# Value products of four heads in 32-column tiles, with the softmax sums as a set of their own

## The chip, the cores and the metric

The kernel runs on one core of one Trainium2 chip. The metric is the device time of one execution in microseconds, the median of the runs.

## What is computed

One gated block of a Flamingo model, on `x` (4 x 512 x 512) and a context of 4 x 1601 x 512, in float32. Cut to what matters:

```python
x = x + jnp.tanh(g_xattn[0]) * mha(layernorm(x), ctx, ctx)     # 16 heads of 32, causal mask of -10000 instead of -inf
x = x + jnp.tanh(g_ffn[0])   * ffn(layernorm(x))
# mha:
scores = jnp.einsum('bhqd,bhkd->bhqk', qh, kh) / math.sqrt(hd)
scores = jnp.where(ki <= qi + (Sk - Sq), scores, -10000.0)
out = jnp.einsum('bhqk,bhkd->bhqd', softmax(scores), vh)
# ffn: rows and weights are rounded to 8-bit floats with a scale per row
t = silu(qx @ qwg.T * scales) * (qx @ qwu.T * scales)           # 512 -> 1408
y = quantized(t) @ qwd.T * scales                                # 1408 -> 512
```

## The kernel before

**The units of work.** The four batches with four groups of four heads each make 16 head groups (`gg`, `GALL = 16`; `NG` = 4 groups a batch, `GH` = 4 heads a group). Keys come in 13 tiles of 128 (`NT`, the last has 65), queries in one row of 512 columns. A group has 26 steps (`STEPS`); in one step the engines do, for one key tile and two heads, the scores (`scores`, L842, with the causal masks of the late tiles at L848), the exps (`exps`, L632, ScalarE) and, two steps later (`LAG = 2`), the value products (`values`, L866). Steps 0 to 12 are the first head pair, 13 to 25 the second. Late key tiles (t = 9 to 12) need fewer query columns: 449, 321, 193, 65.

**Scores** are products of 97 rows: the keys and queries of a head are split in a high and a low 16-bit part, and stacked by DMA (`put_heads`, L335 and L336, 24 copies a group from `kTh`, `kTl`, `qTh`, `qTl`), with a row that holds the shift, minus the maximum of the query's scores (`put_shift`, L340, row `mrow`). The scores of the two heads go to PSUM banks 0 and 1, each in two halves of 64 key columns (`HALVES`), so that two matmuls with 64 columns each share the array. The second use of a bank waits for the exp that reads it (`ex_done`).

**Values** are 32-bit products: the values of a head and a column of ones (33 columns, `VW`), times the exps; the ones give the sum of the softmax. The two heads of a step write partitions 0 to 32 and 64 to 96 of bank 2 or 3. After 13 steps `out_copy` (L622) copies the 97 rows to `oT`, `out_turn` (L823) transposes them, and `join_out` (L1099 to L1112, VectorE) adds the masked part and divides; `add_update` (L460, GpSimd) adds it to `xs`. That is done twice a group, at steps 4 and 17 of the counts that follow.

**The shift** needs the maximum of every score ahead of time. So with each step goes a maximum job for a later group (`max_turn`, L780, two heads of 32 rows at once, masks at L785; `AHEAD = 6`), reduced by VectorE (`max_reduce`, L1069). Its keys are prepared by transposes (`stage_turn`, L767 and L759, at steps 10, 13 and 19), a cast (`stage_high`, L592) and a subtraction (`stage_low`, L1060). The masked values' sums are the suffix products (`suffix_turn`, L808 to L813, step 8).

**The feed-forward part** goes along in the same steps: first the quantization of the weights (`weight_*`, in groups 0 to 3), then, from group 4, one tile of 128 rows per group: transposes at step 20, four up products (`up_turn`, L887) at steps 22, 24, 0 and 2, the hidden transposes (L898) at 12 and the down product (`down_turn`, L910) at 14.

**What sets the order.** Every engine runs its own program over the same step counter `at`; the place of a job in it is written out by hand:

```python
for at in range(END):                       # TensorE, before
    ...                                     # stage_turn, out_turn, suffix_turn, max_turn, shift_turn
    if gg < GALL:
        scores(pe, gg, u)
    if LAG <= at < LAST + LAG:
        values(pe, (at - LAG) // STEPS, (at - LAG) % STEPS)
    ...                                     # row tiles, weights
```

Maximum, stage, suffix, turn, row tile and weight jobs share two bank pairs (banks 4 to 7) in the order in which they are numbered; `free_slot` makes a job wait for whoever reads the pair's last one (`dve_free`, `act_free`). SP issues all loads and copies in one queue.

Of the kernel before, what the change touches and what calls it, by code (L numbers as in the profile page):

```python
# [5 lines left out]
def flamingo_gated_block(nc, x_d, ctx_d, gx_d, gf_d, wg_d, wu_d, wd_d, didx_d, out_d):  # L6
# [9 lines left out]
    P = 128  # L16
# [13 lines left out]
    VW = HD + 1  # L30
# [10 lines left out]
    NP = 6  # L41
    LAG = 2
# [6 lines left out]
    HALVES = ((0, P // 2), (P // 2, P))  # L49
    assert IT * P == I and DT + QT == NT - 1  # L50
# [113 lines left out]
    with ExitStack() as ctx:  # L164
# [26 lines left out]
        vf = sb("vf", [P, NT, H, VW])  # L191
        ksrc = sb("ksrc", [P, NT, P])
        xlg = sb("xlg", [P, QT, P])
        kTh, kTl = sb("kTh", [P, 2, SK], f16), sb("kTl", [P, 2, SK], f16)
        qTh, qTl = sb("qTh", [P, 2, S], f16), sb("qTl", [P, 2, S], f16)
# [5 lines left out]
        pr = sb("pr", [P, NP, S])  # L201
        oT = sb("oT", [P, S])
# [12 lines left out]
        cmb = sb("cmb", [P, QT, 2, HD])  # L215
        upd = sb("upd", [P, QT, 2, HD])
        den = sb("den", [P, 2, QT, 2])
# [12 lines left out]
        t_q = (t_q0[:, :], pr[:, 0:2, :].rearrange("p a n -> p (a n)").bitcast(bf16)[:, 0:I])  # L230
        t_T = (t_T0[:, :], pr[:, 2:4, :].rearrange("p a n -> p (a n)").bitcast(bf16)[:, 0:I])
# [37 lines left out]
        gate_mm, gate_th, ps_clear = sem("gate_mm"), sem("gate_th"), sem("ps_clear")  # L269
# [3 lines left out]
        dve_s, ones_in, vones_in = sem("dve_s"), [sem("ones_in0"), sem("ones_in1")], sem("vones_in")  # L273
# [10 lines left out]
        o_ev, o_tr, upd_ready, xs_done = sem("o_ev"), sem("o_tr"), sem("upd_ready"), sem("xs_done")  # L284
# [11 lines left out]
        def unit(gg, u, j):  # L296
            return 2 * (gg * STEPS + u) + j

# [29 lines left out]
        def put_heads(sp, gg, i):  # L328
            s = gg % 2
            if gg >= 2:  # L330
                sp.wait_ge(qk_mm, unit(gg - 2, i * NT + NT - 1, 1) + 1)
            for r in (2 * i, 2 * i + 1):
                rows = slice(HD * r, HD * r + HD)
                for part in range(3):
                    sp.dma_start(kst[s][HD * part:HD * part + HD, r, :], (kTh, kTl, kTh)[part][rows, s, :]).then_inc(stk[s][r], 16)  # L335
                    sp.dma_start(qst[s][HD * part:HD * part + HD, r, :], (qTh, qTh, qTl)[part][rows, s, :]).then_inc(stk[s][r], 16)  # L336
# [11 lines left out]
        def _(sp):  # L348
# [9 lines left out]
            for i in range(PAIRS):  # L358
                put_heads(sp, 0, i)
# [7 lines left out]
            for i in range(PAIRS):  # L367
                put_heads(sp, 1, i)
            for gg in range(GALL):
# [10 lines left out]
                if g == NG - 1 and b + 1 < B:  # L380
                    for t in range(4):
                        load_values(sp, b + 1, t)
# [3 lines left out]
                if g == NG - 1 and b + 1 < B:  # L386
                    for t in range(4, 8):
# [3 lines left out]
                if g == NG - 1 and b + 1 < B:  # L391
                    load_values(sp, b + 1, 8)
                    load_values(sp, b + 1, 9)
                if gg + 2 < GALL:
                    put_heads(sp, gg + 2, 1)
                if g == NG - 1 and b + 1 < B:
# [58 lines left out]
        def add_update(pool, pp):  # L455

            b, h = pp // (NG * PAIRS), 2 * (pp % (NG * PAIRS))
            cols = slice(h * HD, (h + 2) * HD)
            pool.wait_ge(upd_ready, pp + 1)
# [33 lines left out]
        def _(pool):  # L493
# [22 lines left out]
            nc.gpsimd.memset(vf[:, :, :, HD:VW], 1.0).then_inc(vones_in, 1)  # L516
            pool.wait_ge(consts, 15)
            pool.wait_ge(vones_in, 1)
# [99 lines left out]
        def out_copy(act, pp):  # L618
            act.wait_ge(pv_done, 2 * (pp + 1) * NT)
            if pp >= 1:  # L620
                act.wait_ge(o_tr, pp)
            nc.scalar.copy(oT[0:64 + VW, :], ps[0:64 + VW, 2 + pp % 2, :]).then_inc(o_ev, 1)  # L622

        def exps(act, gg, u):
            t = u % NT
            kn, q0 = KT[t][1], Q0[t]
            for j in range(2):
                n = unit(gg, u, j)
                act.wait_ge(qk_mm, n + 1)
                if n >= NP:  # L630
                    act.wait_ge(pv_done, n - NP + 1)
                nc.scalar.activation(pr[0:kn, n % NP, q0:S], ps[0:kn, j, q0:S], ACT.Exp, scale=SCALE).then_inc(ex_done, 1)  # L632

# [56 lines left out]
        def _(act):  # L690
# [12 lines left out]
            for at in range(END):  # L703
                gg, u = divmod(at, STEPS)
                if gg + 2 < GALL and u in STAGE_AT:
                    stage_high(act, gg + 2, STAGE_AT[u])
                if gg < GALL:
                    exps(act, gg, u)
                if turned_at(at + 2) is not None:
                    out_copy(act, turned_at(at + 2))  # L710
# [26 lines left out]
        def free_slot(pe, job):  # L737

            before = before_in_bank[job]
            if before is None:  # L740
                if banks[job] < 4:
                    pe.wait_ge(ex_done, 2 * LAST)
                    pe.wait_ge(o_ev, GALL * PAIRS)
# [53 lines left out]
        def suffix_turn(pe, gg):  # L797
# [9 lines left out]
            for a, e in HALVES:  # L807
# [471 lines left out]
```

## Time and profile before

| | |
|---|---|
| median of 3 runs | 1160.27 us (1158.86 to 1160.71) |
| profiled execution | 1161.19 us, its span 1159.4 us |
| mean granted TensorE clock | 0.949 of full speed |
| TensorE (PE) busy | 970.5 us, 7770 instructions |
| VectorE (DVE) | 859.7 us, 1438 |
| ScalarE (ACT) | 656.5 us, 1343 |
| GpSimd (POOL) | 332.1 us, 350 |

The busy time of an engine is the time in which at least one of its instructions runs; matmuls overlap, so a busy PE need not be at its peak. A 32-bit matmul stands in the trace as two instructions. The groups begin some 65 us after the start and end near 1041 us; after that come the last row tiles alone.

### The profile page before, as it was taken

To read this page: it belongs to the slowest core of one execution; us is meant where nothing else is said; L and a number is where in the kernel's file an instruction comes from. 1 tells how busy PE (TensorE), PEld (TensorE's weight loads), DVE (VectorE), ACT (ScalarE), POOL (GpSimd) and SP (SyncE) were. 2 spreads that over 40 slices of the span, in tenths; PEclk is the share of its full clock that TensorE was granted. 3 is DMA by queue.
4 is the path that set the end of the run, shared out by engine and by line. 5 is a ranking of instruction groups with operands and counts; after the bars stand their busy time and mean duration, and the time that the engine had idled before them with its cause. 6 is when DMAs were issued, how large, how long until landed. Compare 5 with 4: busy or idle time off the path is not lost.

```text
span 1159.4 us, 21085 instructions
## 1 busy us (share of the span) xinstructions
PE 970.5 (84%) x7770; PEld 399.4 (34%) x7770; DVE 859.7 (74%) x1438; ACT 656.5 (57%) x1343; POOL 332.1 (29%) x350
## 2 busy tenths in 40 slices
PE   4588889888879989999889999998899999984344
PEld 2233333333323334343334333333333343432222
DVE  7768789887747888777677877787778786446764
ACT  2165567675646666666556666665566666753321
POOL 3012323332101414132323232222314132443343
PEclk9998899999989999999999999999999999996766
DMA  7942423230572221114812121218421110000000
GB/s 147 154 122 69 115 66 93 66 86 26 112 88 57 66 57 39 53 43 83 124 41 60 63 61 36 51 41 115 70 61 35 27 41 10 2 10 10 10 10 19
DMA packets 155119, 70.69 MB, mean 61 GB/s; under 512 B 111032, under 2 KB 142856, under 8 KB 155016
## 3 DMA queue, kind: packets, MB, share of 16 engines
q1 hardware_dynamic: 153256, 63.57, 26.5%
q0 software_dynamic: 1760, 5.77, 1.8%
q8 instruction: 62, 1.02, 0.4%
q14 instruction: 41, 0.34, 0.1%
HBM read 39.08 MB, written 4.19 MB: 37 GB/s over the span
## 4 chain that ended last, share of the span: by engine, by line
PE 42%; DVE 36%; issue 10%; ACT 4%; POOL 4%; DMA 2%; SPq 1%; POOLq 0%; DVEq 0%; ACTq 0%
DVE mch L1069 17%; PE ps L866 13%; PE ps L842 8%; PE ps L887 6%; PE ps L780 5%; PE ps L910 3%; DVE ff L985 2%; DVE ff L981 2%; DVE ff L989 2%; PE ps L785 2%; ACT pr L632 1%; DVE upd L1112 1%; DMA qst<-mrow 1%; PE ps L848 1%; DVE cmb L1102 1%
## 5 line engine op out<-in xcount | busy, mean ns | idle before, releaser
L632 ACT ACTIVATE pr<-ps 128x512 f32<-128x512 f32 (+4 forms) x832 | 397.2, 530 | 250.0 <-PE ps L842 125.1
L1069 DVE TENSOR_REDUCE mch<-ps 128x2 f32<-128x1024 f32 (+4 forms) x416 | 432.3, 1056 | 69.2 <-PE ps L780 32.8
L866 PE MATMUL ps<-pr,vf 128*33 128x512 f32 (+4 forms) x1664 | 380.6, 537 | 0.0
L842 PE MATMUL ps<-qst,kst 97*64 97x512 f16 (+4 forms) x1600 | 250.5, 371 | 18.0 <-DMA qst<-mrow 11.4
L780 PE MATMUL ps<-kTh,qTh 32*128 32x512 f16 (+4 forms) x832 | 156.2, 373 | 59.2 <-DVE mch L1069 40.7
L780 PEld LDWEIGHTS ps<-kTh,qTh 32*128 32x128 f16 x832 | 39.5, 92 | 279.0 <-DVE mch L1069 106.9
L842 PEld LDWEIGHTS ps<-qst,kst 97*64 97x64 f16 (+1 forms) x1600 | 77.3, 111 | 108.0 <-ACT pr L632 57.4
L866 PEld LDWEIGHTS ps<-pr,vf 128*33 128x33 f32 (+1 forms) x1664 | 86.8, 113 | 56.6 <-issue 4.9
L1141 DVE SCALAR_TENSOR_TENSOR ff<-ps,scs,wsb 128x352 f32<-128x352 f32 x56 | 32.6, 583 | 73.1 <-PE ps L887 73.1
L448 POOL TENSOR_TENSOR t_q<-ff 128x768 bf16<-128x768 f32 (+1 forms) x28 | 47.4, 1694 | 100.1 <-DVE ff L989 100.1
L887 PE MATMUL ps<-wgu,t_T 128*64 128x352 bf16 x768 | 66.5, 316 | 0.0
L429 POOL TENSOR_TENSOR ff<-ff,wsb 128x352 f32<-128x352 f32 x48 | 46.0, 957 | 64.0 <-DVE ff L1141 64.0
L1060 DVE TENSOR_TENSOR kTl<-ps,kTh 128x1024 f16<-128x1024 f32 (+1 forms) x32 | 31.7, 992 | 41.0 <-ACT kTh L592 40.8
L848 PE MATMUL ps<-maskT,idb 128*64 128x128 bf16 (+2 forms) x576 | 61.7, 214 | 0.0
L989 DVE TENSOR_TENSOR ff<-ff 128x512 f32<-128x512 f32 (+3 forms) x66 | 55.0, 833 | 2.1
L659 ACT ACTIVATE ff<-ps,scs 128x352 f32<-128x352 f32 x48 | 26.6, 554 | 52.2 <-PE ps L887 52.2
L453 POOL TENSOR_TENSOR xs<-xs,ff 128x512 f32<-128x512 f32 x14 | 17.8, 1273 | 132.1 <-DVE ff L1179 132.1
L887 PEld LDWEIGHTS ps<-wgu,t_T 128*64 128x64 bf16 x768 | 44.3, 111 | 32.6 <-issue 20.8
L460 POOL TENSOR_TENSOR xs<-xs,upd 128x256 f32<-128x256 f32 x32 | 24.0, 749 | 107.9 <-DVE upd L1112 107.9
L433 POOL TENSOR_TENSOR ff<-ff 128x352 f32<-128x352 f32 x48 | 51.7, 1078 | 3.8
L489 POOL TENSOR_TENSOR cw<-w,count 128x16 f32<-128x16 f32 x16 | 3.9, 245 | 165.9 <-ACT w L615 165.9
L785 PE MATMUL ps<-idb,maskT 128*64 128x128 bf16 (+2 forms) x640 | 47.1, 229 | 0.0
(151 smaller groups left out, 1198.2 us busy)
## 6 DMA issues: line engine op xcount, KB each, us to landing
kst<-kTh SPq DMA_DIRECT2D x128, 100.1 KB, 2.2
ksrc<-in_ctx SPq DMA_DIRECT2D x16, 768.0 KB
vf<-in_ctx SPq DMA_DIRECT2D x48, 256.0 KB, 5.1
kst<-kTl SPq DMA_DIRECT2D x64, 100.1 KB, 2.2
xs<-in_x SPq DMA_DIRECT2D x16, 256.0 KB, 4.8
qst<-qTh SPq DMA_DIRECT2D x128, 32.0 KB, 1.9
out<-xs SPq DMA_DIRECT2D x16, 256.0 KB, 2.0
ff<-in_L_ffn_w_down SPq DMA_DIRECT2D x4, 704.0 KB, 4.4
```

The lines of the kernel that those rows point to most:

```text
L429: nc.gpsimd.tensor_tensor(t_u[e][:, cols], t_u[e][:, cols], wsb[:, I + c * CW:I + (c + 1) * CW], ALU.mult).then_inc(gated, 1)
L433: nc.gpsimd.tensor_tensor(t_u[e][:, cols], t_u[e][:, cols], t_g[e][:, cols], ALU.mult).then_inc(gu_ready, 1)
L448: nc.gpsimd.tensor_tensor(t_q[e][:, cols], t_v[e][:, cols], t_m[e][:, cols], ALU.subtract).then_inc(qt_ready, 1)
L632: nc.scalar.activation(pr[0:kn, n % NP, q0:S], ps[0:kn, j, q0:S], ACT.Exp, scale=SCALE).then_inc(ex_done, 1)
L780: last = nc.tensor.matmul(slot(job)[:, 512 * i:512 * i + k1 - k0], qTh[rows, gg % 2, qt * P:(qt + 1) * P], kTh[rows, gg % 2, k0:k1], start ...
L785: last = nc.tensor.matmul(slot(job)[a:e, 512 * i + lo - k0:512 * i + hi - k0], maskT[:, a:e], idb[:, lo - d0:hi - d0], start=False, stop=True)
L842: last = nc.tensor.matmul(ps[a:e, j, q0:S], kst[s][0:ST, r, k0 + a:k0 + e], qst[s][0:ST, r, q0:S], start=True, stop=(t < DT))
L848: last = nc.tensor.matmul(ps[a:e, j, q0:q0 + n_m], idb[:, a:e], maskT[:, m0:m0 + n_m], start=False, stop=True)
L866: nc.tensor.matmul(ps[64 * j:64 * j + VW, 2 + pp % 2, q0:S], vf[0:kn, t, h, :], pr[0:kn, n % NP, q0:S], start=(t == 0), stop=(t == NT - 1) ...
L887: last = nc.tensor.matmul(ps[a:e, bank(job) + side, 0:CW], qxT[:, k, a:e], wgu[:, k, side * I + c * CW:side * I + (c + 1) * CW], start=(k ...
L989: return nc.vector.tensor_tensor(v, v, m, ALU.add)
L1069: nc.vector.tensor_reduce(mch[:, qt, 2 * hp:2 * hp + 2, c], both[:, :, 0:k1 - k0], AX.X, ALU.max).then_inc(dve_free, 1)
```

## The change

Steps alternate between the head pairs: steps 2t and 2t + 1 do key tile t for heads 0, 1 and 2, 3. The value products of key tile t are done for all four heads at once in step 2t + 3, each in 32 columns of the array and without the column of ones, into bank 2. The sums are a set of four products with ones as weights (`prob_sums`), into bank 3, at the start of step 2t + 4. The exps have room for three key tiles of four heads. There is one turn, one join and one update a group (128 columns), at step 4; bank 2 and bank 3 are each copied by ScalarE (`out_copy`, `sums_copy`), now ahead of the exps of their step, and the sums are turned by four small products. Scores, suffix, up and down products are cut in `QUARTERS` of 32 columns; the maximum jobs keep 64-column masks. `kTl` and `qTl` have one buffer instead of two, so `stage_low` waits for the copies of the group before, and all 24 head copies of a group are issued at one place, behind the value loads and the shift row. `dynamic_dma_scratch_size` is set to 2048.

```diff
+    QUARTERS = tuple((P // 4 * i, P // 4 * (i + 1)) for i in range(4))
+    TILE_SLOTS = 3
...
     def turned_at(at):
-        pp, rest = divmod(at - 4, NT)
-        return pp - 1 if rest == 0 and 1 <= pp <= GALL * PAIRS else None
+        gg, u = divmod(at, STEPS)
+        return gg - 1 if u == 4 and 1 <= gg <= GALL else None
+    def values_at(at):
+        gg, u = divmod(at - 3, STEPS)
+        return (gg, u // 2) if u % 2 == 0 and 0 <= gg < GALL else None
+    def added_at(at):
+        gg, u = divmod(at - 4, STEPS)
+        return (gg, u // 2) if u % 2 == 0 and 0 <= gg < GALL else None
...
         def load_values(sp, b, t):
-                last = unit(b * NG - 1, STEPS - NT + t, 1)
-                sp.wait_ge(pv_done, last + 1)
+                sp.wait_ge(pv_done, value_count(b * NG - 1, t))
...
-                if gg + 2 < GALL:
-                    sp.wait_ge(dve_free, dve_count["stage", gg + 2, 0])
-                    put_heads(sp, gg + 2, 0)
...
                 if gg + 1 < GALL:
                     put_shift(sp, gg + 1)
...
                     for t in range(10, NT):
                         load_values(sp, b + 1, t)
+                if gg + 2 < GALL:
+                    sp.wait_ge(dve_free, dve_count["stage", gg + 2, 0])
+                    put_heads(sp, gg + 2)
...
         def exps(act, gg, u):
+            t, i = divmod(u, PAIRS)
+            kn, q0, k = KT[t][1], Q0[t], NT * gg + t - TILE_SLOTS
+            if k >= 0:
+                act.wait_ge(sums_done, k + 1)
             for j in range(2):
...
         def scores(pe, gg, u):
-            i, t = divmod(u, NT)
+            t, i = divmod(u, PAIRS)
...
                 if n >= 2:
                     pe.wait_ge(ex_done, n - 1)
-                for a, e in halves:
+                quarters = [(a, min(e, kn)) for a, e in QUARTERS if a < kn]
+                for a, e in quarters:
...
+        def values(pe, gg, t):
+            pe.wait_ge(ex_done, exp_count(gg, t, PAIRS - 1))
+            for r in range(GH):
+                last = nc.tensor.matmul(ps[HD * r:HD * (r + 1), 2, q0:S], vf[0:kn, t, g * GH + r, :], prob(gg, t, r)[0:kn, q0:S],
+                                        start=(t == 0), stop=(t == NT - 1))
+            last.then_inc(pv_done, 1)
+        def prob_sums(pe, gg, t):
+            for r in range(GH):
+                last = nc.tensor.matmul(ps[HD * r:HD * (r + 1), 3, q0:S], onesf[0:kn, 0:HD], prob(gg, t, r)[0:kn, q0:S],
+                                        start=(t == 0), stop=(t == NT - 1))
+            last.then_inc(sums_done, 1)
...
         def stage_low(dve, gg, part):
+            if gg >= 1 and part == PARTS[0]:
+                for r in range(GH):
+                    dve.wait_ge(stk[(gg - 1) % 2][r], ((gg - 1) // 2 + 1) * STK)
```

The order on TensorE, steps 4 to 6 of a group from 4 on. Before (maximum job L780, scores L842, values L866):

```order
L780 MATMUL ps<-kTh,qTh 128x512 x2
L842 MATMUL ps<-qst,kst 64x512 x4
L866 MATMUL ps<-pr,vf 33x512 x2
L780 MATMUL ps<-kTh,qTh 128x512 x2
L842 MATMUL ps<-qst,kst 64x512 x4
L866 MATMUL ps<-pr,vf 33x512 x2
```

Now (turn L837 and L840, maximum job L795, scores L860, values L878, sums L888):

```order
L837 MATMUL ps<-idf,oT 128x128 x4
L840 MATMUL ps<-idf,oS 128x4 x4
L795 MATMUL ps<-kTh,qTh 128x512 x2
L860 MATMUL ps<-qst,kst 32x512 x8
L795 MATMUL ps<-kTh,qTh 128x512 x2
L860 MATMUL ps<-qst,kst 32x512 x8
L878 MATMUL ps<-pr,vf 32x512 x4
L888 MATMUL ps<-pr,onesf 32x512 x4
L795 MATMUL ps<-kTh,qTh 128x512 x2
```

Values stood behind the scores of every step; now a set of values and a set of sums stand together behind the odd step, and between the even and the odd scores there is only a maximum job.

The same around the key transposes of step 10, before (transposes L767):

```order
L866 MATMUL ps<-pr,vf 33x512 x2
L767 MATMUL ps<-idf,ksrc 128x128 x8
L780 MATMUL ps<-kTh,qTh 128x512 x2
L842 MATMUL ps<-qst,kst 64x321 x2
L848 MATMUL ps<-maskT,idb 64x128 x2
```

and now (transposes L782, masks of the maximum job L800):

```order
L888 MATMUL ps<-pr,onesf 32x512 x4
L782 MATMUL ps<-idf,ksrc 128x128 x8
L795 MATMUL ps<-kTh,qTh 128x512 x2
L860 MATMUL ps<-qst,kst 32x512 x8
L795 MATMUL ps<-kTh,qTh 128x449 x2
L800 MATMUL ps<-idb,maskT 64x128 x4
L860 MATMUL ps<-qst,kst 32x512 x8
L878 MATMUL ps<-pr,vf 32x512 x4
```

The second maximum job behind the transposes, which uses their bank pair, has lost the values ahead of it.

## Rows read from the trace of the kernel before

**Rows 1.** The page: busy time, share and instructions of each engine
```profile
PE 970.5 (84%) x7770; PEld 399.4 (34%) x7770; DVE 859.7 (74%) x1438; ACT 656.5 (57%) x1343; POOL 332.1 (29%) x350
```

**Rows 2.** One stretch: PE, PEld, DVE, ACT, POOL busy (x), PEclk, DMA share, GB/s
```profile
443.00:503.00 60.00, 56.74 (x482) 23.10 (x482) 47.04 (x76) 38.33 (x78) 16.86 (x20) 1.00 0.18 47
```

**Rows 3.** The page's chain that ended last, by engine
```profile
PE 42%; DVE 36%; issue 10%; ACT 4%; POOL 4%; DMA 2%; SPq 1%; POOLq 0%; DVEq 0%; ACTq 0%
```

**Rows 4.** PE timeline: start us, us, engine, line, operation, tiles and forms
```profile
665.67 0.39 PE L780 MATMUL ps<-kTh,qTh 32*128 32x512 f16 x2
665.99 0.62 PE L842 MATMUL ps<-qst,kst 97*64 97x512 f16 x4
666.44 1.03 PE L866 MATMUL ps<-pr,vf 128*33 128x512 f32 x4
667.40 0.55 PE L823 MATMUL ps<-idf,oT 97*128 97x97 f32 x4
667.88 0.39 PE L780 MATMUL ps<-kTh,qTh 32*128 32x512 f16 x2
```

**Rows 5.** PE timeline of masked steps, same columns
```profile
647.44 0.41 PE L842 MATMUL ps<-qst,kst 97*64 97x512 f16 x2
647.71 0.38 PE L842 MATMUL ps<-qst,kst 97*64 97x512 f16 x2
654.55 0.30 PE L785 MATMUL ps<-idb,maskT 128*64 128x128 bf16 x4
654.69 0.26 PE L842 MATMUL ps<-qst,kst 97*64 97x193 f16 x2
```

**Rows 6.** PE timeline around one quarter of a row tile's up product
```profile
681.61 1.36 PE L887 MATMUL ps<-wgu,t_T 128*64 128x352 bf16 x16
682.90 0.39 PE L780 MATMUL ps<-kTh,qTh 32*128 32x512 f16 x2
```

**Rows 7.** PE and ACT timeline of two steps that follow closely
```profile
659.54 0.60 PE L842 MATMUL ps<-qst,kst 97*64 97x512 f16 x4
659.96 2.27 ACT L632 ACTIVATE pr<-ps 128x512 f32<-128x512 f32 x4 [0.31 <-PE ps L842]
660.72 0.79 PE L842 MATMUL ps<-qst,kst 97*64 97x512 f16 x4
661.34 0.28 PE L866 MATMUL ps<-pr,vf 65*33 65x65 f32 x4
```

**Rows 8.** Groups by form: the cast and the subtraction of a 1024-column key part
```profile
L592 ACT CAST kTh<-ps 128x1024 f16<-128x1024 f32 x16 | 16.2, 1013 | 10.0 <-PE ps L767 10.0
L1060 DVE TENSOR_TENSOR kTl<-ps,kTh 128x1024 f16<-128x1024 f32 x16 | 19.6, 1226 | 13.6 <-ACT kTh L592 13.6
```

**Rows 9.** PE timeline, waits that return in every group (idle time in brackets)
```profile
466.55 0.39 PE L780 MATMUL ps<-kTh,qTh 32*128 32x512 f16 x2 [0.76 <-DVE mch L1069]
491.20 0.39 PE L780 MATMUL ps<-kTh,qTh 32*128 32x512 f16 x2 [1.01 <-DVE mch L1069]
526.34 0.39 PE L780 MATMUL ps<-kTh,qTh 32*128 32x512 f16 x2 [0.76 <-DVE mch L1069]
```

**Rows 10.** Waits: us in total, times, longest; and PE group L808 by form
```profile
PE ps L842 <- DMA qst<-mrow: 11.4, 3, 5.7
L808 PE MATMUL ps<-vf,later 128*64 128x512 f32 x64 | 17.1, 611 | 5.1 <-POOL vsum L485 4.0 <-DVE mch L1069 1.1
```

**Rows 11.** SP timeline before the second batch: head copies and shift row
```profile
306.70 0.58 SPq L335 DMA_DIRECT2D kst<-kTh  x1
307.33 0.59 SPq L336 DMA_DIRECT2D qst<-qTh  x1
319.53 1.54 SPq L340 DMA_DIRECT2D qst<-mrow  x1
```

**Rows 12.** PEld group of the up product by form
```profile
L887 PEld LDWEIGHTS ps<-wgu,t_T 128*64 128x64 bf16 x768 | 44.3, 111 | 32.6 <-issue 20.8
```

More of the change, by code:

```diff
@@ L297, in unit, with exp_count, value_count, prob @@
             return 2 * (gg * STEPS + u) + j
+        def exp_count(gg, t, i):
+            return unit(gg, PAIRS * t + i, 1) + 1
+        def value_count(gg, t):
+            return NT * gg + t + 1
+        def prob(gg, t, r):
+            i, j = divmod(r, 2)
+            return pr[:, PAIRS * ((NT * gg + t) % TILE_SLOTS) + i, j, :]
         def load_x(sp, b):
@@ L357, in _ @@
             sp.wait_ge(dve_free, dve_count["stage", 0, 0])
-            for i in range(PAIRS):
-                put_heads(sp, 0, i)
+            put_heads(sp, 0)
             for t in range(3, NT):
@@ L366, in _ @@
             sp.wait_ge(dve_free, dve_count["stage", 1, 0])
-            for i in range(PAIRS):
-                put_heads(sp, 1, i)
+            put_heads(sp, 1)
             for gg in range(GALL):
@@ L380, in _ @@
                 if g == NG - 1 and b + 1 < B:
-                    for t in range(4):
-                        load_values(sp, b + 1, t)
-                if gg + 2 < GALL:
-                    sp.wait_ge(dve_free, dve_count["stage", gg + 2, 0])
-                    put_heads(sp, gg + 2, 0)
-                if g == NG - 1 and b + 1 < B:
-                    for t in range(4, 8):
+                    for t in range(10):
                         load_values(sp, b + 1, t)
@@ L742, in free_slot @@
                     pe.wait_ge(ex_done, 2 * LAST)
[L743 removed]
+                    pe.wait_ge(o_ev, GALL)
+                    pe.wait_ge(sums_ev, GALL)
                 return
@@ L815, in suffix_turn, with out_turn @@
             last.then_inc(suf_mm, 1)
-        def out_turn(pe, pp):
-            job = ("turn", pp)
+        def out_turn(pe, gg):
+            job = ("turn", gg)
             free_slot(pe, job)
-            pe.wait_ge(o_ev, pp + 1)
-            n = 64 + VW
+            pe.wait_ge(o_ev, gg + 1)
             for qt in range(QT):
-                last = nc.tensor.transpose(slot(job)[:, qt * n:(qt + 1) * n], oT[0:n, qt * P:(qt + 1) * P], idf[0:n, 0:n])
+                nc.tensor.transpose(slot(job)[:, qt * P:(qt + 1) * P], oT[:, qt * P:(qt + 1) * P], idf[:, :])
+            pe.wait_ge(sums_ev, gg + 1)
+            for qt in range(QT):
+                last = nc.tensor.matmul(slot(job)[:, S + GH * qt:S + GH * (qt + 1)], oS[:, qt * P:(qt + 1) * P],
+                                        idf[:, :].rearrange("p (h d) -> p h d", h=GH)[:, :, 0], start=True, stop=True)
             last.then_inc(o_tr, 1)
         def scores(pe, gg, u):
-            i, t = divmod(u, NT)
+            t, i = divmod(u, PAIRS)
             k0, kn = KT[t]
@@ L885, in up_turn @@
                 for k in range(DC):
-                    for a, e in HALVES:
+                    for a, e in QUARTERS:
                         last = nc.tensor.matmul(ps[a:e, bank(job) + side, 0:CW], qxT[:, k, a:e],
@@ L940, in _ @@
                 gg, u = divmod(at, STEPS)
+                if added_at(at) is not None:
+                    prob_sums(pe, *added_at(at))
                 if gg + 2 < GALL and u in STAGE_AT:
@@ L952, in _ @@
                     scores(pe, gg, u)
-                if LAG <= at < LAST + LAG:
-                    values(pe, (at - LAG) // STEPS, (at - LAG) % STEPS)
+                if values_at(at) is not None:
+                    values(pe, *values_at(at))
                 for n, k in tiles_at(at):
@@ L1088, in suffix_weigh, with join_out @@
                                     ALU.mult).then_inc(dve_free, 1)
-        def join_out(dve, s, pp):
-            gg, i = divmod(pp, PAIRS)
-            k, n = gg % 2, 64 + VW
-            got = slot(("turn", pp))[:, 0:QT * n].rearrange("p (t n) -> p t n", t=QT)
-            sums = [got[:, :, HD + 64 * j] for j in range(2)]
-            dve.wait_ge(o_tr, pp + 1)
+        def join_out(dve, s, gg):
+            got = slot(("turn", gg))
+            update = upd[:, :, :, :].rearrange("p t h d -> p (t h d)")
+            heads = upd[:, :, :, :].rearrange("p t h d -> p (t h) d")
+            dve.wait_ge(o_tr, gg + 1)
@@ L1096, in join_out @@
             dve.wait_ge(cw_ready, gg + 1)
             dve.wait_ge(dve_free, dve_count["suf", gg])
-            for j in range(2):
-                s.step(nc.vector.tensor_tensor(den[:, 0, :, j], cw[:, k, :, 2 * i + j], sums[j], ALU.add))
-            for j in range(2):
-                h = 2 * i + j
-                ins = nc.vector.tensor_tensor(cmb[:, :, j, :], got[:, :, 64 * j:64 * j + HD], sw[:, :, h * HD:(h + 1) * HD], ALU.add)
-                if j == 0:
-                    s.step(ins)
-            s.settle()
@@ new lines, in join_out @@
+            if gg >= 1:
+                dve.wait_ge(xs_done, gg)
+            s.step(nc.vector.tensor_tensor(update, got[:, 0:S], sw[:, :, :].rearrange("p t n -> p (t n)"), ALU.add))
+            s.settle()
+            nc.vector.reciprocal(den[:, 1, :, :], den[:, 0, :, :]).then_inc(dve_free, 1)
+            dve.wait_ge(dve_free, dve_count["turn", gg])
+            nc.vector.scalar_tensor_tensor(heads, heads, tg[:, 0:1],
+                                           den[:, 1, :, :].rearrange("p t h -> p (t h)").unsqueeze(2).broadcast_to([P, QT * GH, HD]),
```

135 lines of the change are left out of this document (55 added, 80 removed).

## The prediction

> **What bounds the kernel now.** I read the busy times first: TensorE (PE) 970.5 us of the 1159.4 us span, VectorE (DVE) 859.7, ScalarE (ACT) 656.5 [rows 1]. The chain that ended last names PE for 42% and DVE for 36% [rows 3], so the two take turns. The stretch view tells more: in 60 us, just over one head group of the steady part, PE is busy for 56.74 at full clock (1.00, the 2.4 GHz level), DVE for 47.04, ACT for 38.33 [rows 2]. One group takes 526.34 - 466.55 = 59.8 us, by the same wait in two groups that follow each other [rows 9]. So PE sets the pace there, and some 3 us a group are its waits. What counts is therefore what one step puts on PE, and what PE waits for.
>
> **One quiet step now** [rows 4], by the starts: maximum job 0.32 us (665.67 to 665.99), scores 0.45, values 0.96, then the next job: 1.74 us in all. The streams are 512/2.4 = 213 ns for the maximum job, 2 x 213 = 427 for the scores, and 853 for the values, if the 32-bit pass takes twice that for each of two passes and two heads share the array. What is left is about 0.11 us behind the maximum job and behind the values, where the shape of the array tile changes, and 0.03 behind the scores, where it does not. Two steps: 3.48 us.
>
> **What the new tiles save on PE: nothing.** Before, 4 heads x 1 key tile are two value sets of two heads, 2 x 0.853. Now they are one set of four value products and one set of four sums, again 2 x 0.853. Scores, suffix, up and down products are cut in four instead of two, twice the instructions with as many streamed sets. The changes of tile shape per two steps stay at four (sums to maximum, to scores, to maximum, to scores). So the sum is made of what follows, per group of 26 steps and against the profiled execution's 1161.2 us (the median of the three runs is 0.9 lower).
>
> **a. The exps come into the path.** Between the scores of an even step and those of the odd step there are no values any more, only a maximum job, and both steps use the same two score banks. How soon scores can follow scores is seen where the values were short: scores at 659.54 and exps of 1.08 us a pair from 659.96; the next scores start at 660.72, sit there for the second exp, and the values behind them start at 661.34, 1.80 us after the first scores [rows 7]. Without that wait it would be 0.43 + 0.11 + 0.32 + 0.45 = 1.31. A quiet pair then takes 1.80 + values 0.86 + sums 0.96 + maximum 0.32 = 3.94 us against 3.48: **+0.46**. Pairs with an up or down product, with a transpose job in the middle or with narrow late key tiles don't pay it: the row tiles' jobs all fall on even steps, between the two scores. Quiet are steps 4/5, 6/7 and 8/9: +1.4 a group.
>
> **b. Steps 10/11.** The key transposes of step 10 hand their bank pair to a cast of 1.01 us and a subtraction of 1.23 [rows 8]; with the hand-overs it is free some 2.5 us later. The maximum job of step 11 wants that pair. With values in between it came 1.74 later or more; now it stands ahead of everything after 0.85, waits 1.6 us, and the scores of step 11 and the values are queued behind it. In return the present wait of 0.76 at this place [rows 9] goes, since values and sums now stand together ahead of the transposes: +0.9. In steps 12/13 (the hidden transposes and their two copies) and 16/17 (masks) I estimate the same mechanism at +0.7 together, between 0 and 1.5.
>
> **c. One more change of tile shape.** The masks of the maximum jobs keep 64 columns; behind them the scores went on after 0.14 us [rows 5]. Now scores have 32: +0.11 in each of 10 masked jobs: +1.1.
>
> **d. Short instructions.** Two masks of 63 columns cost 647.71 - 647.44 - 0.213 = 57 ns [rows 5], so 28 ns an instruction, weights included, where the stream needs 26 for both. Four of them: 112 ns. For 12 heads with 128-column masks (now 4 in 0.14 us, about 60 ns a head) +0.6, for 4 with 63 +0.2, for the 65-key tile (6 instructions a head for 2) +0.5, narrow values and sums +0.2: +1.5. Below it is 0, if the instructions overlap more. An up product is no such case: a set now has 2 in 147 ns (16 in 1.29 - 0.11) [rows 6], and 4 x 28 = 112 still fits.
>
> **e. Turning the result.** Twice four transposes of 0.48 and a shape change [rows 4], 1.2 us, become four, and four sum turns of two passes each with 128 weight columns: between 8 x 0.03 and 8 x 0.12; I take 0.7, nearest to the transposes that load as many columns: +0.1. DVE's join is done once instead of twice, and at step 4 only; ACT copies as often as before, now ahead of the exps of steps 2 and 3, where up products cover it. If those were gone, it would be 0.6 a copy.
>
> a to e: 1.4 + 0.9 + 0.7 + 1.1 + 1.5 + 0.1 = 5.7 us, in the 11 groups 4 to 14: **+63**. Group 15 has no maximum jobs, so scores follow scores at once and wait longer: **+6**. Groups 0 to 3 carry the weight work, with more PE waits for DVE; there c and d (2.6) and a are half hidden: 2.5 each, **+10**.
>
> **f. What is relieved.** The join no longer stands in DVE's queue around step 17, ahead of the waits near step 21; of the 1.01 [rows 9] most stays, since two maximum jobs now stand close together; I take 0.5 a group: **-5.5**. At the three batch starts PE waits 11.4 us for the shift row and 4.0 for the value sums [rows 10]. The shift row was queued on SP behind value loads and 12 head copies of 0.63 each (306.70 to 307.33), and went out at 319.53 [rows 11]. Now a value tile comes free every two steps from step 3 on, the loads spread over the group, and the head copies stand behind the shift row. I take all of it and half a microsecond more: **-16**. The 24 head copies then start with the new group and take 24 x 0.63 = 15 us, and the new wait of the subtraction in step 10, 23 us into the group (10/26 of 59.8), finds them landed. Late next at these places is ACT's shift copy.
>
> Sum: 1161.2 + 63 + 6 + 10 - 5.5 - 16 = 1218.7; I forecast **1217 us** against the median.
>
> **Rivals.**
> **B, faster (12%).** The relief wins. If ACT's release does not hold the odd scores, that is if they may start within 0.85 us of the even ones, a and b go, and so do d and the extra in groups 0 to 3 and 15. Left are c and e, 1.2 x 11 = 13, less 5.5 and 16, and less the restart of PE after the three stops, some 5: 1161 - 13 = 1148. For it: the waits at the batch starts are real. Against it: rows 7 show the stall in this very kernel.
> **C, PE limited by the number of instructions (12%).** 6817 matmuls become 11425 by the order of the programs. If each of the 4608 added, with its weight load, costs 28 to 30 ns on the path, it is +135 in place of d's 20: 1217 + 115 = 1330; if half do, about 1275. For it: 28 ns is measured only where loads are few. Against it: in the up product 16 loads with a mean of 111 ns, 1.78 us, lie within 1.18 [rows 6, 12], so loads of whole columns hide beside the streams. The Trainium skill (TensorE: Matmul & The Clock Gate, "The mechanism") says that a weight load overlaps running matmuls only if its row group differs. By that rule all 128-row loads here would stand in the path, and this rival would be the likeliest; rows 6 and 12 speak against it.
> **D, four tiles don't run four wide (3%).** No row shows more than two. At two wide each step pays 0.43 for scores and 0.85 for values and sums again; over 416 steps, at a mean width of 0.85 of 512, that is +450: 1670.
> **E, the head copies come late (2%).** If SP is held for over 5 us more, the subtraction of step 10 waits and the maximum jobs behind it, some 3 us a batch start: 1226, within my range.
>
> **Numbers.** The forecast has 71%, its own range is 1165 (d zero, the estimates of b zero, groups 0 to 3 unchanged) to 1260 (b and groups 0 to 3 doubled). The range of 1150 to 1275 takes in the half of C that is milder and the upper edge of B. About 0.2% can be told from no change here. Faster: B, 0.12. Same: 0.02, between B and the low end. Slower: the rest, 0.86.
>
> **What would show it.** a: in steps 4 to 9 scores-to-values 1.8 us apart over the pair, with waits for the exps ahead of the second scores; a pair at 3.9. b: a wait of 1.5 us ahead of the maximum job of step 11. c: 0.25 in place of 0.14 behind masks. d: masks of 4 at 0.11 a head. Groups at 65 us in place of 59.8. f: no wait for the shift row. I am wrong if quiet pairs stay near 3.5 us (B), or if a set of four 512-column scores takes clearly more than 0.22 us (C, D).

## The result and the profile after

The changed kernel takes 1215.57 us (median of 4 runs, 1214.02 to 1219.13) against 1160.49 of the kernel before on the same chips: ratio 1.0481, 95% interval 1.0459 to 1.0502. It is slower by 4.8%; 1217 was forecast.

The page of the profile after, busy times and the engines' shares of the chain:

```profile
span 1211.9 us, 31642 instructions
PE 1010.1 (83%) x13370; PEld 414.7 (34%) x13370; DVE 860.1 (71%) x1309; ACT 650.1 (54%) x1343; POOL 325.9 (27%) x333
PE 55%; DVE 24%; issue 9%; ACT 7%; POOL 4%; DMA 1%; SPq 0%; POOLq 0%; ACTq 0%; DVEq 0%
```

Against [rows 1, 3]: PE has 1.7 times the instructions and only 4% more busy time; its share of the chain rises from 42 to 55%, and DVE's falls from 36 to 24%. The next view is one steady group, from its shift transposes to the next one's (columns as in [rows 2]):

```profile
716.80:780.60 63.80, 57.99 (x824) 23.78 (x825) 47.24 (x68) 37.75 (x78) 16.27 (x17) 1.00 0.17 44
```

A group takes 63.8 us, before it took 59.8 [rows 9]. PE is busy for 58.0, against 56.5 in the old group from 496.80 to 556.60 us: 2.6 of the 4 us are waiting, and scores that sit in the array for an exp count as busy on top of it. Where it waits is in PE's timeline of steps 6 to 11 (start, us, engine, line, operation, tiles, count; idle time before in brackets):

```profile
733.93 1.03 PE L878 MATMUL ps<-pr,vf 128*32 128x512 f32 x8
734.80 1.03 PE L888 MATMUL ps<-pr,onesf 128*32 128x512 f32 x8
735.76 0.39 PE L795 MATMUL ps<-kTh,qTh 32*128 32x512 f16 x2
736.08 0.25 PE L800 MATMUL ps<-idb,maskT 128*64 128x63 bf16 x4
736.26 0.61 PE L860 MATMUL ps<-qst,kst 97*32 97x512 f16 x8
736.81 0.39 PE L795 MATMUL ps<-kTh,qTh 32*128 32x512 f16 x2
737.42 0.89 PE L860 MATMUL ps<-qst,kst 97*32 97x512 f16 x8 [0.23 <-ACT pr L644]
738.14 1.03 PE L878 MATMUL ps<-pr,vf 128*32 128x512 f32 x8
...
742.64 0.61 PE L860 MATMUL ps<-qst,kst 97*32 97x512 f16 x8
743.22 0.39 PE L795 MATMUL ps<-kTh,qTh 32*128 32x512 f16 x2
743.80 0.89 PE L860 MATMUL ps<-qst,kst 97*32 97x512 f16 x8 [0.20 <-ACT pr L644]
744.52 1.04 PE L878 MATMUL ps<-pr,vf 128*32 128x512 f32 x8
...
749.80 0.36 PE L795 MATMUL ps<-kTh,qTh 32*128 32x449 f16 x2 [1.50 <-DVE kTl L1088]
750.09 0.30 PE L800 MATMUL ps<-idb,maskT 128*64 128x128 bf16 x4
750.33 0.62 PE L860 MATMUL ps<-qst,kst 97*32 97x512 f16 x8
```

The reader sees four things. A set of four value products streams in 0.87 us (733.93 to 734.80), and one of four sums in as much: four tiles do run side by side, and each key tile needs two sets as before. From the even scores to the values behind the odd ones it is 1.88 us twice (736.26 to 738.14, 742.64 to 744.52); the odd scores start late and last 0.89, since their second bank waits for the second exp. Ahead of the maximum job of step 11 PE waits 1.50 us for the subtraction. And between masks and scores there are 0.24 us (750.09 to 750.33), where it was 0.14 [rows 5].

### The profile page after: what moved, and what is told of

It is laid out like the page before. It is cut to its first block, busy times and chain, and to the rows that moved or that the text cites. A ratio compares the mean times of both kernels' runs of the same rounds, so it can differ in the third digit from the quotient of the medians.

```text
span 1211.9 us, 31642 instructions
## 1 busy us (share of the span) xinstructions
PE 1010.1 (83%) x13370; PEld 414.7 (34%) x13370; DVE 860.1 (71%) x1309; ACT 650.1 (54%) x1343; POOL 325.9 (27%) x333
## 4 chain that ended last, share of the span: by engine, by line
PE 55%; DVE 24%; issue 9%; ACT 7%; POOL 4%; DMA 1%; SPq 0%; POOLq 0%; ACTq 0%; DVEq 0%
PE ps L878 11%; PE ps L888 11%; DVE mch L1097 10%; PE ps L860 10%; PE ps L795 6%; PE ps L910 5%; ACT pr L644 5%; PE ps L933 3%; PE ps L800 2%; DVE ff L1010 2%; PE ps L782 1%; DVE kTl L1088 1%; DVE ff L1169 1%; ACT kTh L601 1%; DVE ff L1006 1%
## 5 line engine op out<-in xcount | busy, mean ns | idle before, releaser
L860 PE MATMUL ps<-qst,kst 97*32 97x512 f16 (+5 forms) x3264 | 261.9, 364 | 20.5 <-ACT pr L644 14.3
L795 PE MATMUL ps<-kTh,qTh 32*128 32x512 f16 (+4 forms) x832 | 156.8, 374 | 73.2 <-DVE mch L1097 36.0
L878 PE MATMUL ps<-pr,vf 128*32 128x512 f32 (+4 forms) x1664 | 203.1, 559 | 0.0
L888 PE MATMUL ps<-pr,onesf 128*32 128x512 f32 (+4 forms) x1664 | 198.6, 550 | 0.2 <-ACT oS L635 0.2
L795 PEld LDWEIGHTS ps<-kTh,qTh 32*128 32x128 f16 x832 | 39.5, 92 | 270.3 <-DVE mch L1097 125.1
L860 PEld LDWEIGHTS ps<-qst,kst 97*32 97x32 f16 (+1 forms) x3264 | 72.9, 95 | 130.9 <-ACT pr L644 74.8
L888 PEld LDWEIGHTS ps<-pr,onesf 128*32 128x32 f32 (+1 forms) x1664 | 53.2, 113 | 103.1 <-issue 93.5
L910 PE MATMUL ps<-wgu,t_T 128*32 128x352 bf16 x1536 | 66.6, 312 | 0.0
L866 PE MATMUL ps<-maskT,idb 128*32 128x128 bf16 (+3 forms) x1216 | 66.5, 215 | 0.0
L878 PEld LDWEIGHTS ps<-pr,vf 128*32 128x32 f32 (+1 forms) x1664 | 48.4, 114 | 23.3 <-issue 3.0
L910 PEld LDWEIGHTS ps<-wgu,t_T 128*32 128x32 bf16 x1536 | 43.5, 96 | 12.4
L1199 DVE SCALAR_TENSOR_TENSOR ff<-ps,scs,wdb 128x512 f32<-128x512 f32 x14 | 10.5, 751 | 52.0 <-PE ps L933 52.0
```

The costliest lines, as they stand in the source:

```text
L795: last = nc.tensor.matmul(slot(job)[:, 512 * i:512 * i + k1 - k0], qTh[rows, gg % 2, qt * P:(qt + 1) * P], kTh[rows, gg % 2, k0:k1], start ...
L860: last = nc.tensor.matmul(ps[a:e, j, q0:S], kst[s][0:ST, r, k0 + a:k0 + e], qst[s][0:ST, r, q0:S], start=True, stop=(t < DT))
L866: last = nc.tensor.matmul(ps[a:e, j, q0:q0 + n_m], idb[:, a:e], maskT[:, m0:m0 + n_m], start=False, stop=True)
L878: last = nc.tensor.matmul(ps[HD * r:HD * (r + 1), 2, q0:S], vf[0:kn, t, g * GH + r, :], prob(gg, t, r)[0:kn, q0:S], start=(t == 0), stop=( ...
L888: last = nc.tensor.matmul(ps[HD * r:HD * (r + 1), 3, q0:S], onesf[0:kn, 0:HD], prob(gg, t, r)[0:kn, q0:S], start=(t == 0), stop=(t == NT - 1))
L910: last = nc.tensor.matmul(ps[a:e, bank(job) + side, 0:CW], qxT[:, k, a:e], wgu[:, k, side * I + c * CW:side * I + (c + 1) * CW], start=(k ...
```

## Experiments

Each was timed beside the kernel before; ratios are against it. Where a gain or a loss against the changed kernel is given in us, it is a difference of medians.

### The sums behind the even scores

```diff
-                if added_at(at) is not None:          # first in the step
-                    prob_sums(pe, *added_at(at))
...
                     scores(pe, gg, u)
+                if added_at(at) is not None:
+                    prob_sums(pe, *added_at(at))
```

> The set of sums moves from the start of an even step to behind its scores, so that 0.85 us of work lies between the scores of the even and of the odd step; the number of instructions, of streamed sets and of changes of tile shape stays. Theory (the exps came into the path): the pair of steps 6/7 falls from 4.2 to about 3.7 us, the wait of 1.50 us ahead of the maximum job of step 11 to below 0.7, a steady group from 63.8 to 61.5 us, the whole to 1175 us (1165 to 1185). Rival (the loss is in the cut of the products and the tile shapes): nothing of that lies in this order, 1210 us or more.

Measured: 1143.34 us, ratio 0.985 (0.9825 to 0.9876), 72 us less than the changed kernel by a move of one call, and 1.5% faster than the kernel before. A steady group takes 60.1 us. Steps 4 to 6 in its timeline of PE:

```profile
621.80 0.62 PE L860 MATMUL ps<-qst,kst 97*32 97x512 f16 x8
622.25 1.03 PE L888 MATMUL ps<-pr,onesf 128*32 128x512 f32 x8
623.21 0.39 PE L795 MATMUL ps<-kTh,qTh 32*128 32x512 f16 x2
623.53 0.62 PE L860 MATMUL ps<-qst,kst 97*32 97x512 f16 x8
623.97 1.03 PE L878 MATMUL ps<-pr,vf 128*32 128x512 f32 x8
624.94 0.39 PE L795 MATMUL ps<-kTh,qTh 32*128 32x512 f16 x2
```

Scores to scores takes 1.73 us here, with no wait for the exps; a step had 1.74 in [rows 4]. So the pair fell as expected, and the wait of 1.50 at step 11 is gone (in a group of 60 us the maximum jobs wait 1.5 us for DVE in all, at two places). The gain was nearly twice what I expected (72 for 40). By the starts of the groups 48 us of it are in groups 4 to 14, where a full-clock group gives 3.7 us in place of 2.3 and the mean clock rises from 0.98 to 1.00, and 20 us in groups 0 to 3.

### The same order in the kernel before

```diff
-                if LAG <= at < LAST + LAG:
-                    values(pe, (at - LAG) // STEPS, (at - LAG) % STEPS)
+                if at % 2 == 1:
+                    for v in (at - 3, at - 2):
+                        if 0 <= v < LAST:
+                            values(pe, v // STEPS, v % STEPS)
```

with `NP = 8` in place of 6, and the DMA scratch of 2048.

> The kernel before, with its 33-column values, halves and pair order, but the values of two steps together behind the scores of the odd step, as the change places them (buffers for 8 exps in place of 6, and the smaller DMA scratch that the change uses too, to make room). Nothing else of the change is in it. Theory (term a is a matter of the order alone): quiet pairs take 3.9 in place of 3.5 us, with waits for the exps of 0.2 us or more ahead of the odd scores: +2.5 us a group and more, 1200 us (1185 to 1215). Rival (the cut in quarters or the sums' products cost the time): within 5 us of the kernel before.

Measured: 1209.17 us, ratio 1.0415 (1.0373 to 1.0456). With halves, 33-column values and no sums' products, the order costs 49 us (the two more exp buffers and the smaller scratch, which came with it, were not timed by themselves). Two quiet steps of it:

```profile
541.04 0.60 PE L842 MATMUL ps<-qst,kst 97*64 97x512 f16 x4
541.57 0.39 PE L780 MATMUL ps<-kTh,qTh 32*128 32x512 f16 x2
542.12 0.90 PE L842 MATMUL ps<-qst,kst 97*64 97x512 f16 x4 [0.16 <-ACT pr L632]
542.85 1.89 PE L866 MATMUL ps<-pr,vf 128*33 128x512 f32 x8
```

Scores to values 1.81 us, as [rows 7] had it (1.80). PE's waits for the subtraction grow too, from 6.0 to 20.6 us, so it is term b as well as term a. Both experiments together show the two: covered again in the changed kernel they give 72 us back, put into the old one they cost 49.

### The key transposes at step 11

```diff
-    STAGE_AT, SUMS_AT, ... = {10: 1, 13: 2, 19: 0}, 6, ...
+    STAGE_AT, SUMS_AT, ... = {11: 1, 13: 2, 19: 0}, 6, ...
```

> The changed kernel with the key transposes of step 10 at step 11, on every engine. Theory (term b): the maximum job of step 11 has another bank pair, its wait of 1.50 us goes, and the transposes fill the gap between the scores of steps 10 and 11: a steady group from 63.8 to 62.3, the whole 1195 us (1190 to 1202). Rival (the wait is DVE's load, not the place): it turns up as a wait of the maximum jobs of steps 12 or 13, 1210 us or more.

Measured: 1190.69 us, ratio 1.0256 (1.0208 to 1.0303), 25 us less than the changed kernel; a steady group takes 62.4 us. The list of PE's waits of the changed kernel (engine, line, waited for: us in total, times, longest) has

```profile
PE ps L795 <- DVE mch L1097: 36.0, 56, 1.8
PE ps L795 <- DVE kTl L1088: 18.5, 13, 1.9
PE ps L860 <- ACT pr L644: 14.3, 55, 0.5
```

and with the transposes at step 11 the one for the subtraction is no longer among the 60 largest, while the other two stand as they were:

```profile
PE ps L795 <- DVE mch L1097: 37.1, 56, 1.8
PE ps L860 <- ACT pr L644: 14.3, 55, 0.5
```

So the wait of step 11 was a matter of the place. Of its 18.5 us some 3 turned up again ahead of the key transposes, which now wait 3.3 us for DVE's reductions where they waited 0.3.

### Masks of the maximum jobs in quarters

```diff
-                    for a, e in HALVES:        # the masks in max_turn
+                    for a, e in QUARTERS:
```

> The masks of the maximum jobs are cut in quarters of 32 columns too, so the scores behind them need no change of tile shape. Theory (term c): 10 changes a group at 0.09 us go, and 4 more short instructions a job cost nothing, since four masks of 128 columns take 0.06 us in the trace of the changed kernel: 0.9 us a group, 1201 us (1198 to 1207). Rival (term d as forecast, 28 ns an instruction): 8 masks take 0.22 in place of 0.14 us and give most of it back: 1213 us.

Measured: 1207.15 us, ratio 1.0408 (1.0349 to 1.0467). The scores follow the masks sooner, with twice as many masks:

```profile
749.67 0.30 PE L800 MATMUL ps<-idb,maskT 128*32 128x128 bf16 x8
749.80 0.61 PE L860 MATMUL ps<-qst,kst 97*32 97x512 f16 x8
```

0.13 us for eight masks, in place of 0.24 for four and a change of shape. By its groups the gain is 0.95 us in the one that kept full clock, of 62.85 us; but most of its groups take 64.5, at a mean clock of 0.97 (last section). The median, 8 us lower, carries both and lies between the two expectations; its interval allows 1 to 15, so this run alone does not tell them apart. The 0.13 us for eight masks does.

### Scores in halves

```diff
-                quarters = [(a, min(e, kn)) for a, e in QUARTERS if a < kn]
+                quarters = HALVES if kn == P else [(0, kn)]
```

> The scores and their masks go back to two halves of 64 columns; values, sums, up and down products stay in quarters. Half of the added score instructions go; the change of shape behind masked maximum jobs goes (10 a group), and one comes ahead of the values of each of 13 odd steps and of the 6 up and down products. If instructions cost nothing: 0.08 x 19 - 0.09 x 10 = +0.6 us a group, 1225 us. If they cost 28 ns each as term d had it: -1.5 in each group, 1200 us.

Measured: 1248.61 us, ratio 1.0755 (1.0728 to 1.0782). The direction is that of free instructions and costly changes of shape, the size is not: +33 us for the +9 expected.

```profile
690.84 0.89 PE L860 MATMUL ps<-qst,kst 97*64 97x512 f16 x4 [0.21 <-ACT pr L644]
691.66 1.07 PE L878 MATMUL ps<-pr,vf 128*32 128x512 f32 x8
692.54 1.04 PE L888 MATMUL ps<-pr,onesf 128*32 128x512 f32 x8
```

The change of shape ahead of the values shows (0.82 us from scores to values, where it was 0.72), and behind masked maximum jobs it is gone. A group at full clock takes 65.2 us, 1.4 over the changed kernel, where 19 changes more and 10 fewer made me expect 0.6 (0.9 at the 0.10 us a change that is measured here). Further groups take 66.9 and 68.5 at a mean clock of 0.97 and 0.95, and the groups with the weights up to 74.5 at 0.87. The half microsecond a group that is left is not explained.

### The sums on 64 columns

```diff
+            c0 = 0 if t == 0 else S - 64
...
-                last = nc.tensor.matmul(ps[HD * r:HD * (r + 1), 3, q0:S], onesf[0:kn, 0:HD], prob(gg, t, r)[0:kn, q0:S],
+                last = nc.tensor.matmul(ps[HD * r:HD * (r + 1), 3, c0:S], onesf[0:kn, 0:HD], prob(gg, t, r)[0:kn, c0:S],
```

> The sums are taken over all columns for the first key tile only and over the last 64 query columns for the other twelve, so the sums of the other columns are left incomplete; all waits and places stay. It measures what the set of sums costs. By the streams, the 12 sets fall from 8.5 us a group to 1.3. If PE sets the pace with its streams: -7 us a group, 1105 us (1095 to 1125), which is what halving the value sets had saved. Rival (the waits for ACT and DVE set the pace): the streams are partly cover for the exps, and at most half comes out: 1160 us or more.

Measured: 1147.15 us, ratio 0.9892 (0.9862 to 0.9922). 68 us come out of 112 that 16 groups at 7 us would give: between the two expectations. The sets do shrink to 0.22 us, but the maximum jobs then wait longer for DVE (53.2 us in all, for 36.0). A group at full clock takes 58.0 us, 5.8 less than in the changed kernel, where the streams are 7.2 less. So the set of sums is mostly in the path, and by the streams it costs what the values of four heads at once had saved; a kernel with next to no sums' work would only have come near the old one, in this order.

### Where the shift row comes late: two orders of SP in the kernel before

The first puts the 12 copies behind the shift row, at the end of a batch alone:

```diff
-                if gg + 2 < GALL:
+                late = g == NG - 1
+                if gg + 2 < GALL and not late:
                     sp.wait_ge(dve_free, dve_count["stage", gg + 2, 0])
                     put_heads(sp, gg + 2, 0)
...
                     put_shift(sp, gg + 1)
+                if gg + 2 < GALL and late:
+                    sp.wait_ge(dve_free, dve_count["stage", gg + 2, 0])
+                    put_heads(sp, gg + 2, 0)
```

> The kernel before, with one thing moved: in the last group of a batch SP issues the first 12 head copies behind the shift row in place of ahead of the value loads. Theory (term f): the shift row was late because 12 copies of 0.63 us stood ahead of the loads and it; the waits of PE for it, 11.4 us in all, fall below 3, and the time to 1150 us (1146 to 1154). Rival (the queue's data, 256 KB a value tile, hold it up, not the issues): the waits stay above 8 us, no change beyond 2 us.

Measured: 1171.56 us, ratio 1.0103 (1.0072 to 1.0135): 1% slower where 1150 us was expected, a miss. Two lines of its list of waits say why:

```profile
POOL vsum L486 <- DMA vf<-in_ctx: 47.0, 4, 15.5
PE ps L812 <- POOL vsum L489: 29.0, 3, 11.9
```

The waits for the shift row, 11.4 us in [rows 10], are gone from the list. In their place PE waits 29 us for the value sums, for 4.0 before. The sums need the last three value tiles, and these stand behind all 24 copies in both orders. At the first batch start they go out at the same time, in the old kernel and in this one:

```profile
333.21 3.39 SPq L321 DMA_DIRECT2D vf<-in_ctx  x3
333.01 3.39 SPq L321 DMA_DIRECT2D vf<-in_ctx  x3
```

There the suffix products start at 341.47 us before and at 341.22 now. What was lost is the cover: PE had stood 5.7 us for the shift row and then 1.4 for the sums, and now it stands 11.9 for the sums. So it is not that the tiles came "now behind 24 copies", as the next expectation puts it; they had been late all along. The second order takes the change's own: all value loads and the shift row first, then both halves of the copies.

```diff
-                if gg + 2 < GALL:
+                if gg + 2 < GALL and not late:
                     put_heads(sp, gg + 2, 1)
                 ...                                   # loads of value tiles 10 to 12
+                if gg + 2 < GALL and late:
+                    sp.wait_ge(dve_free, dve_count["stage", gg + 2, 0])
+                    put_heads(sp, gg + 2, 0)
+                    put_heads(sp, gg + 2, 1)
```

> The kernel before, with SP's order at the end of a batch as the change has it: all value loads and the shift row first, then all 24 head copies. In the run that moved only 12 copies the waits for the shift row were gone, but the last three value tiles, now behind 24 copies, made the value sums late by 29 us. Theory (term f, both waits together): waits for the shift row and the value sums fall from 15.4 to below 3 us, 1160 becomes 1144 us (1140 to 1149). Rival (the head copies are then late for the step 10 subtraction or the next group's scores): 1155 us or more.

Measured: 1139.89 us, ratio 0.9825 (0.9785 to 0.9865): 20 us off the old kernel by its DMA order alone, 4 more than expected. Among its 60 largest waits there is none of PE for the shift row or the value sums. Groups 4 to 14 as one stretch, in the old kernel and in this one (columns as in [rows 2]):

```profile
313.00:984.80 671.80, 621.10 (x5111) 248.72 (x5110) 511.52 (x846) 411.34 (x839) 176.71 (x192) 0.98 0.29 58
312.40:962.20 649.80, 612.14 (x5110) 245.98 (x5108) 511.12 (x846) 411.26 (x839) 176.50 (x192) 1.00 0.29 60
```

Of the 22 us less, 13 are waits of PE (50.7 to 37.7). The other 9 are busy time with the same instructions: before, the clock fell four times, three of them at these waits (5.7 and 3.1 us for the shift row, 2.1 for the value sums; mean 0.98), and now it does not (1.00). Term f is shown for the batch starts, both the shift row and the value sums, and with the falls of the clock it is worth more than its waits.

### Versions that beat both

The sums behind the even scores and the masks in quarters together:

> Both edits that helped: the sums behind the even scores, and the masks of the maximum jobs in quarters. If the changes of shape are on the path (term c), another 1.0 us a group against the run with the sums moved: 1128 us (1124 to 1133). Rival: with the exps covered, maximum jobs wait for DVE's reductions anyway, and the gain is below half: 1138.

Measured: 1132.21 us, ratio 0.9753 (0.9725 to 0.9781), 11 us below the run with the sums moved alone. Steady groups take 59.3 us, 0.8 less than there (1.0 was expected): changes of shape are on the path once the exps are covered. With the key transposes at step 11 as well:

> The best so far (sums behind the even scores, all masks in quarters, 1132 us), with the key transposes at step 11 too. There the pair of steps 10/11 already has the sums between its scores, and the wait at step 11 is small, so the theory (the place mattered only because nothing covered it) expects no more than 0.3 us a group either way: 1132 us (1127 to 1137). Rival (the place itself costs, as it did with a wait of 1.5 us): 1115 us.

Measured: 1130.28 us, ratio 0.9736 (0.9699 to 0.9773). The same within the noise, as expected: the place of the transposes mattered only while nothing stood between the scores. It has the lowest median here, 2.6% below the old kernel.

## Why the prediction was right

The time came out within 2 us of the forecast, by the mechanism that was named; but the parts were off in both directions, so the total is better than its parts, and that is luck. By the start of the shift transposes in each group, the end of group 3 came at 331.3 us (before: 313.0), that of group 14 at 1032.2 (984.8), and the rest took 179.7 us (174.6). So the 52.5 us of the span split into 18.3 up to group 3, 29.1 in groups 4 to 14, and 5.1 behind. Forecast were 10; 63 - 5.5 - 16 = 41.5; and 6. A steady group was put at 5.7 - 0.5 = 5.2 us more and takes 4.0.

**a. The exps in the path: right.** A quiet pair was put at 3.94 us. Steps 8/9 take 6.38 from values to values, with 2.46 of suffix products in it: 3.92. Read in the same way, without the turn and the masks, steps 4/5 and 6/7 take 4.01 and 4.03. The stall itself, read from one place in the old trace [rows 7], was 1.80 us from scores to values and is 1.88. The two experiments that move the order confirm it in both kernels.

**b. Steps 10/11: right.** A wait of 1.6 us was forecast and is 1.50, and of the 0.76 of step 10 [rows 9] nothing is left. In steps 12/13 PE waits 1.10 for ScalarE's copies, where it waited 0.70, and in 16/17 the exps hold the odd scores for some 0.5: 0.9 together, for the 0.7 forecast.

**c. The change of shape: right in its price.** 0.24 for 0.14 us behind masks, and gone when the masks have the same shape. Over the ten masked jobs of a group it comes to 0.8 us for 1.1, since two of them, ahead of the 65-key tile, had a change of shape before too.

**d. Short instructions: wrong.** This is the largest mis-sized term of groups 4 to 14. The 57 ns of two masks were what two score products and their masks take together, less 213 ns for the scores. The old trace has a row between the two of [rows 5]:

```profile
647.68 0.20 PE L848 MATMUL ps<-maskT,idb 128*64 128x63 bf16 x2
```

The scores took 0.24 us (647.44 to 647.68), and the two masks 0.03 (to 647.71). The timeline after, with four such masks:

```profile
764.84 0.40 PE L860 MATMUL ps<-qst,kst 97*32 97x512 f16 x4
765.07 0.21 PE L866 MATMUL ps<-maskT,idb 128*32 128x63 bf16 x4
765.10 0.39 PE L860 MATMUL ps<-qst,kst 97*32 97x512 f16 x4
```

Four masks with their weights take 0.03 us too, where the stream of 63 columns needs 0.026; four of 128 columns take 0.06 (584.67 to 584.73) for 0.053. So four matmuls cost what two cost, some 8 ns each with the load and not 28, and the term of 1.5 us a group, 16 in groups 4 to 14, was about nothing. That also settles rival C: 4608 matmuls more cost next to nothing, 640 instructions more (masks in quarters) went with less time, and 2304 fewer (scores in halves) with more. The rule from the Trainium skill cited there (TensorE: Matmul & The Clock Gate, "The mechanism"), that weight loads overlap only matmuls of other row groups, is not what this trace shows: the loads of four masks of 128 rows run from 584.59 to 584.70 us, beside score products of 97 rows that start at 584.58 and 584.67. Rival D falls by the 0.87 us of a set of four.

**Groups 0 to 3: too low, by the clock.** 18 us came for 10. Groups 1 to 3 as one stretch, before and after (columns as in [rows 2]):

```profile
123.52:313.00 189.48, 164.29 (x1267) 64.66 (x1266) 154.98 (x280) 127.34 (x282) 60.39 (x62) 0.98 0.30 77
121.26:331.30 210.04, 182.96 (x2056) 71.17 (x2056) 155.06 (x260) 126.72 (x282) 60.03 (x59) 0.91 0.29 79
```

They take 20.6 us more; group 0 takes 1.4 less. PE waits hardly longer (27.1 for 25.2 us), but is busy for 18.7 more, and the mean clock falls from 0.98 to 0.91. With only two levels that is some 38 us at 1.2 GHz, for 8 before. If PE worked all through it, half of the difference is lost, up to 15 us, and some 6 are left for the stalls: 2 a group, near the 2.5 of the forecast. So "half hidden" is not refuted; the term that failed is the clock in these groups, which the sum put at nothing. What brings it down there is open. It falls less in the old kernel with the values' places changed (mean 0.93 over these groups) and with the sums moved (0.95), and more with the scores in halves (0.87, 0.93 and 0.88), so it goes with the time lost on PE, but it was not tried by itself.

**f. The relief: right at the batch starts, absent elsewhere.** 16 us were forecast. The groups at the three batch starts took 63.3, 66.4 and 68.0 us and take 60.9, 66.0 and 66.0. With the 4.0 that every group loses, that is a relief of 17, and in the old kernel the same DMA order gave 20 us. The 24 copies behind it were never late (rival E). The other part, 5.5 us for a shorter wait near step 21, did not come: it is 1.20 us, for 1.01 [rows 9].

**e and what is left.** The turn adds 1.38 us, for 1.3. But each of the two turns before had added only the 0.48 between its start and the next job [rows 4], since values to turn takes the 0.96 of values to maximum job; so e is +0.4 a group, not +0.1. Read in this way the terms add up to some 4.5 us for the 4.0 of a steady group (1.5 + 0.7 + 0.9 + 0.8 + 0 + 0.4 + 0.2); the half microsecond between is not taken apart. The runs close like this: 1160, less 20 for the DMA order, plus 11 for c, gives 1151 for a kernel whose exps are covered, and 1143 was measured with the sums moved. The 8 us between may be the join that DVE does once instead of twice; that was not tried, and it is a difference between runs of different rounds.

Rival B, faster, failed where it was expected to, at the odd scores. But its other half was true: the relief was there, and with one call moved the kernel is faster than before.

## What to carry to other kernels

Before two short stages are merged into one longer one, look at what the merged pieces had covered: here each value set stood between two uses of the same PSUM banks, and gave the exps their time. A set of work on the busiest engine can be worth as much by its place as by its length (moving the sums gave 72 us, cutting most of them away 68), and the place costs nothing to change. And an order of DMA issues that comes with another change should be timed alone: here it hid 20 us of gain in a change that lost 55. And a stall can cost more than its wait: look at the busy time of the same instructions and at the mean clock as well.

## What was not expected of the hardware

Four 32-column matmuls with four weight loads passed in 0.03 us (63 columns) and 0.06 us (128 columns), in one stream with the scores around them: what the columns alone need, whether two or four matmuls carry them.

The clock fell behind short waits. In groups 4 to 14 of the changed kernel it did so seven times: three times behind the wait of 1.2 us at step 21, twice behind the 1.50 of step 11, and twice behind waits of 0.3. In most other groups it did not, at the same places. One of them in PE's timeline:

```profile
516.47 0.39 PE L795 MATMUL ps<-kTh,qTh 32*128 32x512 f16 x2 [1.19 <-DVE mch L1097]
...
517.20 1.61 PE L878 MATMUL ps<-pr,vf 128*32 128x449 f32 x8
518.58 1.72 PE L888 MATMUL ps<-pr,onesf 128*32 128x449 f32 x8
520.24 0.60 PE L795 MATMUL ps<-kTh,qTh 32*128 32x512 f16 x2
```

From values to sums of 449 columns it is 1.38 us and from there to the next job 1.66, for 0.75 and 0.86 in a group at full clock. That group had two such falls and took 67.1 us for 63.8. Ahead of this one PE had done four short transposes and then waited. With the masks in quarters, where the wait is 1.32 us, five of eleven groups have a spell at this place and three more at another, and what the edit gained in them went into it. In the versions without the stalls of steps 6 to 11 (the sums moved, with or without the other edits) and in the old kernel with the value loads first, these groups show no fall at all, at a mean clock of 1.00. Which wait brings a fall and which does not, these runs do not tell.
